# A two-layer decoder on one core: the maxima of the attention as rows of the queries, the mixture's shares by a broadcast from memory, and the order of the work written anew

## What is computed

```python
scores = einsum('bhqd,bhkd->bhqk', q, k) / sqrt(D)      # causal, then softmax over k
attn = softmax(scores); op = einsum('bhqk,bhkd->bhqd', attn, v)

scores = softmax(xt @ Wg.T)                # 16 experts in 4 groups
# the best 2 groups, in them the best 4 experts; combine[t, e] = score or 0
h = silu(einsum('td,eid->eti', xt, W1)) * einsum('td,eid->eti', xt, W3)   # 176 inner rows an expert
y = einsum('etd,te->td', einsum('eti,edi->etd', h, W2), combine)
z = silu(xt @ Ws1.T) * (xt @ Ws3.T) @ Ws2.T                               # shared, 352 inner rows
```

## Time and profile before

| | |
|---|---|
| median of 3 runs | 535.6 us (534.62 to 535.94) |
| the profiled execution, its own time | 534.2 us |
| its span, first to last instruction | 532.4 us |
| PE busy, share of the span | 493.6 us, 93% |
| PE weight loads | 362.3 us, 68% |
| DVE busy | 396.9 us, 75% |
| ACT busy | 345.2 us, 65% |
| POOL busy | 190.4 us, 36% |
| granted PE clock, mean | 0.987 |
| chain that ended last | PE 67%, DVE 16%, ACT 9%, issue 4%, POOL 3%, DMA 1% |

### The profile page before, as it was taken

How to read it: one execution, slowest core, us unless ns; L and a number is a source line. 1 busy time by engine, 2 the same in 40 slices (tenths; PEclk the granted TensorE clock), 3 DMA queues, 4 the chain that set the end, 5 groups by cost and what they waited for, 6 DMA issues and landing times.

```text
span 532.4 us, 11834 instructions
## 1 busy us (share of the span) xinstructions
PE 493.6 (93%) x4694; PEld 362.3 (68%) x4721; DVE 396.9 (75%) x917; ACT 345.2 (65%) x601; POOL 190.4 (36%) x288
## 2 busy tenths in 40 slices
PE   5869887899999999999999999999999999999985
PEld 3424533567778788877887878777777676678654
DVE  2787997879677988548996587644876568689984
ACT  5666744766676236894269845588535874976796
POOL 3129986741340150330004072613052221032562
PEclk9987999899999999999999999999999999999999
DMA  8502443220000001000000020200000300000001
GB/s 290 216 0 63 149 162 114 71 81 1 1 3 1 2 10 71 1 2 2 1 1 2 1 80 3 81 1 1 1 1 2 120 1 1 1 2 2 0 27 55
DMA packets 5943, 21.66 MB, mean 41 GB/s; under 512 B 896, under 2 KB 3072, under 8 KB 5120
## 3 DMA queue, kind: packets, MB, share of 16 engines
q1 hardware_dynamic: 5888, 20.91, 11.6%
HBM read 19.86 MB, written 1.05 MB: 39 GB/s over the span
## 4 chain that ended last, share of the span: by engine, by line
PE 67%; DVE 16%; ACT 9%; issue 4%; POOL 3%; DMA 1%; ACTq 0%; DVEq 0%; POOLq 0%
PE ps L1072 24%; PE ps L1106 15%; PE ps L820 4%; DVE nmx L2524 3%; PE ps L951 3%; PE ps L844 2%; PE ps L880 2%; PE ps L1082 2%; PE ps L928 2%; PE ps L875 2%; PE ps L798 2%; PE ps L970 1%; PE ps L931 1%; DVE hl L2642 1%; PE ps L1152 1%
## 5 line engine op out<-in xcount | busy, mean ns | idle before, releaser
L2631 DVE TENSOR_TENSOR hs<-hs,ps 128x512 f32<-128x512 f32 (+1 forms) x68 | 45.2, 668 | 40.0 <-PE ps L1072 27.3
L1952 ACT ACTIVATE hs<-ps 128x512 f32<-128x512 f32 (+1 forms) x68 | 39.4, 581 | 51.1 <-PE ps L1072 42.7
L2524 DVE TENSOR_REDUCE nmx<-ps 128x2 f32<-128x512 f32 (+1 forms) x96 | 60.4, 681 | 7.2 <-PE ps L880 7.1
L556 POOL TENSOR_TENSOR ve<-mv,half 128x2 f32<-128x2 f32 x24 | 7.7, 322 | 149.0 <-DVE mv L2418 149.0
L1106 PE MATMUL ps<-w2h,hh 128*128 128x256 f16 x200 | 54.7, 274 | 0.7 <-DVE hl L2642 0.5
L1106 PE MATMUL ps<-w2h,hl 128*128 128x256 f16 x200 | 54.6, 273 | 0.0
L1106 PE MATMUL ps<-w2l,hh 128*128 128x256 f16 x200 | 54.6, 273 | 0.0
L1959 ACT ACTIVATE hh<-hs 128x512 f16<-128x512 f32 (+1 forms) x52 | 31.5, 611 | 34.5 <-DVE hs L2637 23.3
L2642 DVE TENSOR_TENSOR hl<-hs,hh 128x512 f16<-128x512 f32 (+1 forms) x52 | 40.1, 779 | 8.9 <-ACT hh L1959 8.6
L1911 ACT ACTIVATE pk<-ps 128x512 f32<-128x512 f32 x64 | 34.6, 597 | 12.1 <-PE ps L931 9.6
L1072 PE MATMUL ps<-yah,w1h 128*128 128x256 f16 x200 | 38.4, 274 | 1.9 <-DVE hs L2631 1.9
(11 more groups left out here) (249 smaller groups left out, 1338.5 us busy)
## 6 DMA issues: line engine op xcount, KB each, us to landing
stage<-in_w SPq DMA_DIRECT2D x12, 800.0 KB, 4.3
tstage<-in_tern SPq DMA_DIRECT2D x4, 1024.0 KB, 4.9
cs<-in_ctxT SPq DMA_DIRECT2D x1, 1024.0 KB, 9.4
cd<-in_ctxT SPq DMA_DIRECT2D x1, 1024.0 KB, 4.8
out_x<-xs SPq DMA_DIRECT2D x4, 256.0 KB, 2.2
sels<-in_sel SPq DMA_DIRECT2D x1, 800.0 KB, 9.8
w0s<-in_w SPq DMA_DIRECT2D x1, 768.0 KB, 7.0
xs<-in_x SPq DMA_DIRECT2D x1, 768.0 KB, 8.2
```

Of the source, the lines that this page charges most:

```text
L1952: act.activation(hs[:, n % 3, 0:w], ps[:, gate_bank(n), 0:w], ACT.Silu).then_inc(e_sil.sem, 1)
L2524: dve.tensor_reduce(nmx[:, int(n % 3 > 0), first + par:first + 2 * heads:2], ps[:, max_bank(it, n) + par, :].rearrange("p (h k) -> p h k", ...
L2631: TT(hs[:, n % 3, 0:w], hs[:, n % 3, 0:w], ps[:, up_bank(n), 0:w], ALU.mult).then_inc(e_hb.sem, 1)
```

## The change

Two things are computed in another way, and the lists of all five engines are written in another order.

**Maxima.** Rows 48 and 49 of the keys (112 and 113 for odd heads) hold the constant 64, and the same rows of the queries hold the maxima over 64, high and low half, so that one product over 50 rows gives scores less maximum. `selh`'s product in `scores_exp` is gone. The way of the maxima: PE transposes `nmx` in float32 to 16 rows, ACT copies them to `mh`, DVE makes the rest `ml`, and SP moves them by four small transfers an iteration, each from 8 partitions to one row of `qT` (8 pieces of 512 bytes). `scores_exp(it, 0)` waits for all four.

**Shares.** The inner rows are reordered (on the host, in the weights): the first 16 tiles are the first 128 rows of one expert each, the next 6 hold 8 rows of all 16 experts (partition 16r + e), the last 3 the shared part. For the first 8 pairs a share is one row for all partitions of a tile: SP writes the transposed shares to memory (16 rows of 1 KB), waits for it, and reads them back, one transfer a pair, to all 128 partitions (256 KB) into one of three buffers `shs`. For the next 3 pairs `cT` itself, now 128 rows with the experts repeated, is the share. The last 2 pairs need none. `spread` is gone. `times_share` now comes before `times_up` and takes both operands from SBUF; `up(n+1)` waits for `silu_of(n)` only.

```diff
 def maxima_turned(it):      # PE
-    pe.wait_ge(m_lo.sem, m_lo.at(it, 1))
+    pe.wait_ge(mx_ok.sem, mx_ok.at(it, 12))
...
-        mm = pe.transpose(bank16(0, BF16)[:, j * P:(j + 1) * P],
-                          mtok[:, j, :, :].rearrange("p a c -> p (a c)"), idb[:, :])
+        mm = pe.transpose(ps[0:H, 0, j * P:(j + 1) * P], nmx[:, j, :, :].rearrange("p r a -> p (r a)"), ident)
 def scores_exp(it, n):      # PE
     if n == 0:
-        pe.wait_ge(m_ok.sem, m_ok.at(it, 1))
+        pe.wait_ge(d_m.sem, d_m.at(it, 64))
...
-        for part in range(2):
-            for par in range(2):
...
+        for par in range(2):
+            r = 64 * par
+            mm = pe.matmul(ps[:, first + par, i * width:(i + 1) * width],
+                           kT[r:r + 50, h // 2, kt * P:(kt + 1) * P], qT[r:r + 50, h // 2, q0:S],
 def up(n):                  # PE
-    pe.wait_ge(e_hc.sem, n)
+    pe.wait_ge(e_sil.sem, n)
-def spread(n):
...
-def maxima_high(it):        # ACT
...
 def maxima_turned(it):      # ACT
-    act.activation(mT[:, :], bank16(0, BF16)[:, 0:S], ACT.Copy).then_inc(m_ok.sem, 1)
+    if it:
+        act.wait_ge(d_m.sem, d_m.at(it - 1, 64))
+    act.activation(mh[0:H, :], ps[0:H, 0, 0:S], ACT.Copy, scale=1.0 / M_UNIT).then_inc(m_ok.sem, 1)
 def maxima_low(it):         # DVE
-    for j in range(JT):
-        last = TT(mtok[:, j, :, H:2 * H], nmx[:, j, None, :].to_broadcast([P, 2, H]), mtok[:, j, :, 0:H], ALU.subtract)
+    dve.scalar_tensor_tensor(ml[0:H, :], ps[0:H, 0, 0:S], 1.0 / M_UNIT, mh[0:H, :],
+                             ALU.mult, ALU.subtract).then_inc(m_lo.sem, 1)
 def router_experts(b):      # DVE, ctk in float32, the experts repeated 8 times
-    link(TT(cw[:, :, :], mk[:, :, 0:E0], mr[:, :, 0:E0], ALU.subtract))
-    link(dve.tensor_copy(ctk[:, :, 0:E0], cw[:, :, :]))
-    TT(ctk[:, :, E0:2 * E0], cw[:, :, :], ctk[:, :, 0:E0], ALU.subtract).then_inc(ctk_ok.sem, 1)
+    for j in range(JT):
+        last = TT(ctk[:, j, :].rearrange("p (r e) -> p r e", e=E0), mk[:, j, None, 0:E0].to_broadcast([P, 8, E0]),
+                  mr[:, j, None, 0:E0].to_broadcast([P, 8, E0]), ALU.subtract)
 def times_share(n):         # DVE
-    dve.wait_ge(e_hb.sem, n + 1)
-    dve.wait_ge(e_c.sem, n + 1)
-    TT(hs[:, n % 3, 0:w], hs[:, n % 3, 0:w], ps[:, gate_bank(n), 0:w], ALU.mult).then_inc(e_hc.sem, 1)
+    if kind == "hash" or p >= MASKED_PAIRS:          # 11
+        return
+    dve.wait_ge(e_sil.sem, n + 1)
+    if p < SHARE_PAIRS:                              # 8
+        dve.wait_ge(d_sh[u % 3].sem, 16 * (u // 3) + 16)
+        share = shs[:, u % 3, :].rearrange("p (k t) -> p k t", k=2)
+    else:
+        share = cT[:, b % 2, None, :].to_broadcast([P, 2, S])
+    TT(mine, mine, share, ALU.mult).then_inc(e_hc.sem, 1)
 # SP
+def maxima_rows(it):
+    for half, row in ((mh, 48), (ml, 49)):
+        sp.wait_ge(...)                              # m_ok for mh, m_lo for ml
+        for par in range(2):
+            r = 64 * par + row
+            sp.dma_start(qTs[it % 2][r:r + 1, :, :], half[8 * par:8 * par + 8, :]).then_inc(d_m.sem, 16)
+def shares_out(b):
+    sp.wait_ge(cw_ok.sem, b + 1)
+    sp.dma_start(shares[b].rearrange("(e t) -> e t", e=E0), cT[0:E0, b % 2, :]).then_inc(d_shw.sem, 16)
+    sp.wait_ge(d_shw.sem, 16 * b + 16)
+def shares_in(b, p):                                 # u = 8 b + p
+    if u >= 3:
+        sp.wait_ge(e_hc.sem, ...)                    # times_share of load u - 3
+    sp.dma_start(shs[:, u % 3, :], shares[b:b + 1, 2 * S * p:2 * S * (p + 1)].to_broadcast([P, 2 * S])).then_inc(...)
```

More of the change, by code:

```diff
@@ L52 @@
 MASKED = -1e30
+M_UNIT = 64.0
 MAX_BANKS = (2, 4, 0)
@@ L1122, in outs @@
                 first, count = MIXED.get(it, (0, 0))
-                if k < count:
-                    spread(first + k)
                 if 0 < k <= count and (k < MOE_PAIRS or not is_mixture(it)):
@@ L1375, in _ @@
+            project(3, 1)
+            up(6)
+            back(2, 0)
+            down(3)
+            scores_exp(2, 5)
+            values(2, 2)
+            gate(7)
             up(7)
-            back(2, 0)
-            scores_exp(2, 5)
+            down(4)
+            down(5)
             stack(3, 0)
             stack(3, 1)
-            down(4)
-            values(2, 2)
+            gate(8)
+            down(6)
+            scores_max(3, 0)
+            stack(3, 2)
+            up(8)
             values(2, 3)
-            spread(7)
@@ L1541, in _ @@
+            gate(33)
+            logits(3)
+            down(30)
             values(4, 0)
             values(4, 1)
-            gate(32)
-            up(32)
+            stack(5, 2)
             scores_exp(4, 4)
-            stack(5, 2)
-            down(30)
-            gate(33)
-            spread(32)
-            scores_exp(4, 5)
             stack(5, 3)
             down(31)
-            up(33)
-            spread(33)
+            scores_exp(4, 5)
+            gate(34)
+            back(4, 0)
@@ L1600, in _ @@
             up(41)
-            values(5, 0)
-            down(39)
-            scores_exp(5, 2)
-            spread(41)
-            gate(42)
-            tail_turned(4)
-            up(42)
-            spread(42)
-            down(40)
-            scores_exp(5, 3)
-            gate(43)
+            up(42)
+            down(39)
+            scores_exp(5, 1)
+            tail_turned(4)
+            gate(42)
+            scores_exp(5, 2)
+            down(40)
+            down(41)
+            first_turn(6)
@@ L1612, in _ @@
+            gate(43)
+            scores_exp(5, 3)
+            project(6, 0)
+            up(43)
+            values(5, 0)
             values(5, 1)
-            first_turn(6)
             scores_exp(5, 4)
-            up(43)
-            project(6, 0)
-            back(5, 0)
             gate(44)
+            down(42)
             project(6, 1)
-            spread(43)
+            up(44)
+            up(45)
+            gate(45)
             scores_exp(5, 5)
-            down(41)
-            down(42)
@@ L2837, in _ @@
             output_low(1)
-            times_up(0)
-            times_share(0)
             maxima_low(2)
@@ L3135, in _ @@
             normal(7, 1)
+            times_up(61)
             inner(0, 1)
```

1298 lines of the change are left out of this document (620 added, 678 removed).

## The result

The changed kernel took 528.3 us (median of 4 runs, 524.8 to 530.5) beside 535.1 us of the kernel before on the same chip: a ratio of 0.988, interval 0.984 to 0.991. Measured a second time it was 526.7 (6 runs) beside 533.9, ratio 0.988, interval 0.985 to 0.991. So the change gives 6.5 us by the ratio (6.8 and 7.2 by the medians). The forecast was 519, a gain of 16.6 us; the measured time lies in its range, near the end.

A forecast was written before the change was run, and what follows sets the result against it. PE was taken to bound the mixture and most of what follows. From the profiled 534.2 us, 11.0 and 7.8 were subtracted, 1.4 and 1.1 added, giving 517.9, or 519 as the median of runs; the range was 509 to 531.

The forecast's parts named there:

- What bounds: Whole kernel by stretch: PE bounds the mixture, busy 275.1 of 280 us, so work taken off it there saves its time.
- spread, 11.0 us: Mixture: dropping 100 `spread` products of 0.11 us each from PE saves 11.0 us.
- selh, 7.8 us: `scores_exp`: dropping the `selh` products saves 1.3 us in each of iterations 2 to 7, 7.8 us in all.
- Float32 transpositions (+1.4) and 50 rows (0 to 1): PE: 32-bit transpositions of maxima and shares add 1.4 us; products over 50 rows cost nothing, bounds 0 and 1 us.
- Other engines in the mixture: Mixture: DVE loses about 5 of 204 us, ACT loses `maxima_high`; both stay below PE, costed at nothing.
- The front: Before the first `down`: DVE gains 5 us, late transfers give it back, net +1.1 us, bounds -5 to +6.
- Shares of samples 1 to 3, maxima of 3 to 6: Mixture: share transfers take 5.8 us but are issued pairs ahead, maxima have `down` and `gate` ahead of scores; no cost.
- Iteration 7: Last maxima to scores grows from 2.4 to some 5 us, covered by other PE work; no cost, bounds 0 and 2.6.
- The tail: Feed-forward end: new order with 14 fillers as before, taken as 0, bounds -3 and +3 us.
- B: Rival, mixture: DVE binds in places and shares SBUF access with POOL, 8 us more DVE work; 527, up to 532; chance 0.24.
- C: Rival, mixture: waits in SP's in-order list leave the share transfers open at four starts, 23 us, so 542; chance 0.10.
- A: Rival, start: small transfers take 1.5 us and the front's 5 us gain stays; 513, to 509; chance 0.15.

The follow-up runs named there:

- the kernel without all three: The kernel before without the `selh` products, without `spread` and without `times_share`: 521.3 us, ratio 0.977.
- the kernel with SP's list mended: The changed kernel with the first shares' write ahead of iteration 2's maxima rows and three read-backs ahead of the first ternary piece: 529.1 us, ratio 0.990.

## Why the prediction was wrong, step by step

**What bounds.** "An instruction taken off PE is worth its time in the second stage": this step failed. From 275 of 280 us of busy PE it was taken that PE's waits stay at 5 us. Leaving out the products alone gave 10.5 of 18.8 us, and PE's standing in the mixture rose from 4.9 to 10.2 us. The busy share says who works, not how far behind the others are; DVE at 18.5 of 20 us was in the text. My reading is that the lists of three engines were laid so that all arrive nearly together: take some 0.36 us a pair (18.8 over 52) from one, and the other two, and the fixed order, set part of the pace. Shown is that leaving out DVE's share product helps (2.5 us in the old lists, 7.9 in the new, where PE then stands for 1.4 us); that it brings back all of the 8.3 us is disproved by the kernel without all three (521.3).

**spread, 11.0 us.** Its time on PE is right, its worth alone is 5.9. **selh, 7.8 us**: right on PE, since a unit from its first product to PE's next instruction shrank from 0.55 to 0.33 us in the timelines (36 units from iteration 2 on); alone worth 6.6. Together 10.5.

**Float32 transpositions (+1.4) and 50 rows (0 to 1).** Not measured alone. Two transpositions in float32 take 0.21 to 0.25 us in the new timelines (0.25 forecast). A unit of 50 rows takes 0.33 us, as two steps of 0.11 and the gap of 0.11 that the 48-row units had as well; the rows cost nothing.

**Other engines in the mixture: "Both stay below PE, so I cost this at nothing."** Failed too. The new order of share and up product was seen ("`gate(n+1)` waits for two DVE steps instead of one") and costed at nothing since other work stands between. In the old lists it costs 5.6 us. In the new ones `gate` stands 5.1 us for DVE, but with the order turned back other waits take its place and 1 us or nothing is gained. What costs there is the share product itself: without it 7.9 us go.

**The front.** The last maxima of iteration 2 ended at 114.0, not 112. From there to the scores it was 5.8 us (5.1 forecast): PE's transposition came 1.1 us late, and four issues took 2.6 us and not 1.8. The first `down` came at 130.4, not 127. The reason given (shares behind the ternary piece) is only a part of it: the write did wait, but the silu behind three units of exponentials and DVE's context product were as late, and the kernel with SP's list mended shows no gain. And the step's weight was too high: 4.3 us won there were worth nothing at the end.

**Shares of samples 1 to 3, maxima of 3 to 6: no cost.** Right within 2 us: without the transfers the time changes by 0 to 2 us, and `gate` does not stand for DMA. **Iteration 7: 4.7 us from its last maxima (441.9) to its scores (446.6), "some 5" forecast**, with 0.4 us of it standing: right. **The tail** of the feed-forward was 1.8 us shorter (34.2 us from its first down product, 36.0 before), inside 0 and -3.

**The rivals.** B (DVE takes over in places, 527) is nearest in time and in kind, but for another cause. It priced 8 us for access to SBUF, and that too low: rows 12 show 0.63 us more on an instruction of 256 columns that takes 0.42 alone, which for 0.7 us would be 1.0 more, 44 x 0.27 x 1.0 = 12 us. What came are 2 us: the 44 share products took 32.1 us, 0.68 us each (as before) would be 30. In the changed kernel 41 of them take 0.66 to 0.69 us; the three others take 1.03, 1.19 and 1.66 us, each beside a working POOL. So that the time lies within the range, in the part that was there for B, is in part luck. DVE's groups by form in the changed kernel (busy time, mean ns of one, idle time before and its releasers):

```profile
L2604 DVE TENSOR_TENSOR hs<-hs,ps 128x512 f32<-128x512 f32 x64 | 43.7, 685 | 13.3 <-ACT hs L1928 6.1 <-PE ps L1111 3.0
...
L2624 DVE TENSOR_TENSOR hl<-hs,hh 128x512 f16<-128x512 f32 x48 | 39.6, 837 | 9.2 <-ACT hh L1935 8.8
L2619 DVE TENSOR_TENSOR hs<-hs,shs 128x512 f32<-128x512 f32 x32 | 22.9, 714 | 22.1 <-ACT hs L1928 19.0 <-issue 1.6 <-DMA shs<-shares 0.8
```

Two SBUF inputs take 0.71 and 0.84 us on average, one from PSUM 0.69. The rule of the Trainium skill, "GPSIMD Engine Reference", Specifications, that instructions with two SBUF inputs contend with GpSimd, agrees with the three long share products and with rows 12 in kind. C (SP starves the mixture) did not come: the share product waited 0.8 us in all for DMA. A fell: the start came later, not earlier. The read-back lands in 3.3 us (median); the row of 2.2 was too low for it. The Trainium skill's fit in "DMA: Bandwidth & Descriptors", two cost components, gives an estimated 2.6 us and is low as well.

**Of the 8.8 us that are missing** in the profiles, no sum can be made from these runs. The kernel without the products lacks nearly as much (18.8 less 10.5 = 8.3), but not in the same place: its stretch from the first `down` to the last up product is 6.4 us shorter than before, that of the changed kernel 11.7. So the new lists bring out more of PE's gain in the mixture than the old ones, and the start (3.5 us later) and the end (0.6 us longer in one profile, 1.6 shorter in the other) give part of it back. How much of the step from 6.4 to 11.7 is the place of the share, `up` that waits for less, or the order was not tried apart.

## What to carry to other kernels

Where the busiest engine works 98% of a stretch and the next ones 62 to 73% under a carefully laid order, a saving on the busiest need not be worth its time (here 56% of it in the old order): leave the work out of the old kernel first and measure what that order gives for it. When work moves from one engine to another's chain, look at which wait of the next turn it now stands in front of, above all with in-order lists; and expect an order laid out for one placement to hide, or to eat, the gain of the other. An earlier start of one chain can be worth nothing if the engine that feeds it is then late for the next one, as DVE was here.

## What the hardware showed unexpectedly

- After a stand of 2.3 us PE was granted the lower of its two clocks (1.2 GHz) for some 6 us in the midst of the mixture; with fillers in that stand it was not. After a stand of 3.1 us (POOL taking over `inner_low`) it ran at the lower clock for 3 us. A stand of 1.25 us ahead of the scores of iteration 2 left the clock at 1.00. So moving work earlier can cost PE's clock.
- A row of the queries that 8 partitions send to one takes SP 0.66 us to issue, and an ordinary transfer 0.44. The 16 KB write lands in 1.4 us (median of four), but the first of them, behind the 1 MB ternary piece, was waited for until 123.8, 4.6 us after its issue; put ahead of the piece, it had landed when SP came to the read-backs at 118.65.
- The broadcast read of one 2 KB row to 128 partitions (256 KB) lands in 3.3 us (median; 3.0 to 8.2) where 256 KB from SBUF to memory take 2.2.
